# A graph block's edge sums: the overlap of two edge runs zeroed by one VectorE product per group instead of ScalarE copies

## The chip, the cores and the metric

The kernel runs on one core of a Trainium2 chip. The metric is the device time of one launch in microseconds (us), as the median of several runs. The core has five engines with queues of their own: TensorE (PE; its weight loads are shown as PEld), VectorE (DVE), ScalarE (ACT), GpSimd (POOL) and SyncE (SP). Each engine executes its own list of instructions strictly in order, and they meet at semaphores.

## The reference

There are 6250 nodes with 256 features and 106,250 edges with 96 features; the edges are sorted by their target node. For each node, the sum, the maximum and the mean of its edges' features are taken, put beside its normalised features and a global vector, and fed to a two-layer perceptron:

```
h = jnp.maximum(_layernorm(x, axis=-1), 0.0)
col = edge_index[1]
out1 = segment_sum(edge_attr, col)
cnt = segment_sum(ones, col)
out2 = where(cnt > 0, segment_max(edge_attr, col), 0)
out3 = out1 / maximum(cnt, 1.0)
z = concatenate([h, out1, out2, out3, u[batch]], axis=1)
y = relu(z @ W1 + b1) @ W2 + b2
out = x + (y + h)
```

## The kernel before, in words

**Tiles and groups.** The nodes are dealt to 49 tiles of 128 (one node to each partition), each partition's nodes being sorted by their number of edges, so that all 128 nodes of tile i have between LOW[i] and CAP[i] edges. A tile's edges are fetched by GpSimd as two runs, each with one indirect DMA (line 309): the first LOW edges of each node (k1 slots of 96 floats), and its last CAP - LOW edges (k2 slots). For a node with fewer than CAP edges the second run begins inside the first: those slots are the overlap. A table `mk` (128 x 49 x 20) holds 1 for slots of the second run that are new and 0 for slots of the overlap. For the maximum the overlap does no harm; for the sum it must be zeroed. One or two tiles with equal LOW and CAP form a group; there are 27 groups, 0 to 26. Edges lie in `ell` (all k1 + k2 slots), the zeroed copy of the second run in `es`; each has two buffers, by the group's parity, and both are named `work` in the trace.

**The overlap.** `mask` (lines 394 to 406) runs on ScalarE: for each of the n*k2 slots of a group (n tiles) one ACTIVATE Copy of 128x96 from `ell` to `es`, with the slot's column of `mk` as its scale (line 404). That makes 435 instructions, cut into pieces that stand between other work of ScalarE. The last one of a group signals `masked`.

**The trees.** `tree_head` on VectorE waits for `masked` (line 738) and adds the first run to `es` (line 743; in four tiles whose first run is shorter, line 748 also clears values for the maximum). `tree_mid` and `tree_tail` halve both buffers (line 754) until one sum and one maximum are left, in `cat`; the tail signals `tree_done`. GpSimd's `gather_group` waits for `tree_done` of group g before it issues the gathers of group g + 2 into the same buffer.

**The rest.** The 49 tiles form 14 batches of 2 to 4 tiles (1, 2 or 3 groups). ScalarE's `norm` and `means` fill the rest of `cat`. For each tile k of a batch TensorE transposes `cat` (line 523), ScalarE copies the result to `inh` (`in_hi`, line 440) and VectorE takes the rounding remainder `inl` (`in_lo`, line 843). TensorE then works at eight chunks (m = 0 to 7) of the hidden layer for the batch, `layer1` and, two chunks later, `layer2`; between them ScalarE does `relu` (lines 413 and 415) and VectorE `lo` (line 839).

**The order.** It is written by hand. A stage s has eight steps m. In it TensorE computes the chunks of batch s and, at the ends of chunks 2, 3, 5 and 6, transposes tiles 0, 1, 2 and 3 of batch b = s + 1; they are called k0 to k3 here. Transposes of one tile wait for `in_lo` of the tile before. VectorE at step m begins with `lo` of chunk m - 1 and then does: m = 0 and 1, mid and tail of the batch's first group; m = 2, `output` (line 865) and the head of the second group; m = 3, `in_lo` of tile 0 and mid; m = 4, `in_lo` of tile 1, tail, and the head of a third group; m = 5, the third group's mid and tail, and `moments` (line 810) of a batch ahead; m = 6, `in_lo` of tile 2 and `residual` (line 856); m = 7, `in_lo` of tile 3, `scales` (lines 822 to 832) and the head of the next batch's first group. ScalarE's pieces of `mask` come after `relu` of m = 0, 3, 4, 5, 6 and 7; for the next batch's first group they begin at m = 4 or 5, ahead of the step at which VectorE needs them.

The program has a branch for data that do not fit LOW and CAP (lines that begin with `general > 0`), which isn't taken.

Of the kernel before, what the change touches and what calls it, by code (L numbers as in the profile page):

```python
# [13 lines left out]
P = 128  # L14


def gnn_block(nc, x, dst, edge, u, W1, b1, W2, b2, out):
# [173 lines left out]
    x_in = [S(f"x_in{i}") for i in range(XS)]  # L191
    stored = [S(f"stored{i}") for i in range(XS)]
    ell_in = [S(f"ell_in{i}") for i in range(2)]
    masked, tree_done = S("masked"), S("tree_done")
    var_ready, std_ready, ln_done = S("var_ready"), S("std_ready"), S("ln_done")
    h_done, outs_done, over_done, trans_done = S("h_done"), S("outs_done"), S("over_done"), S("trans_done")
    hiT_done, loT_done, rem_hi, rem_lo = S("hiT_done"), S("loT_done"), S("rem_hi"), S("rem_lo")
# [33 lines left out]
    with nc.Block() as block:  # L231
# [136 lines left out]
        def _(act):  # L368
# [22 lines left out]
                act.wait_ge(var_ready, b + 1)  # L391
                act.activation(sd_[:, b % 2, 0:n], ve[:, b % 2, 0:n], ACT.Sqrt).then_inc(std_ready, 1)

            def mask(g, piece=0, pieces=1):

                a, n, k1, k2, _, _ = groups[g]
                if g == 0:
                    act.wait_ge(mask_ready, 1)
                if piece == 0:
                    act.wait_ge(ell_in[g % 2], ell_count(g))  # L400
                for at in range(n * k2 * piece // pieces, n * k2 * (piece + 1) // pieces):
                    j, e = at // k2, at % k2
                    src = (j * (k1 + k2) + k1 + e) * F
                    last = act.activation(es[g % 2][:, at * F:(at + 1) * F], ell[g % 2][:, src:src + F], ACT.Copy, scale=mk[:, a + j, e:e + 1])  # L404
                if piece == pieces - 1:
                    last.then_inc(masked, 1)

            def relu(C):
                cols = width(C // HC) * P
                m = C % HC  # L410
# [42 lines left out]
                    if k == width(b) - 1:  # L453
                        rem_in_hi(b)

            mask(0)
            root(0)
            for s in range(-1, NB):
                b = s + 1
                n, gs, ahead = width(b) if b < NB else 0, groups_in(b), groups_in(b + 1)  # L460
                for m in range(HC):
                    if m == 1:
                        for k in range(min(n, 1)):
                            norm(b, k)
                    if m == 2:
                        for k in range(1, min(n, 2)):
                            norm(b, k)
                        if n:
                            means(gs[0])
                    if m == 3:  # L470
                        in_high(b, 0)
                        for k in range(2, n):
                            norm(b, k)
                    if m == 4:
                        in_high(b, 1)
                    if m == 5 and len(gs) > 1:
                        means(gs[1])
                    if m == 6:
                        if len(gs) > 2:
                            means(gs[2])  # L480
                        in_high(b, 2)
                    if m == 7:
                        in_high(b, 3)
                    if s >= 0:
                        if s * HC + m == 0:
                            act.wait_ge(bias_set, 1)
                        relu(s * HC + m)
                    if m == 0 and len(gs) > 1:
                        mask(gs[1], 1, 2)
                    if m in (3, 4) and len(gs) > 2:  # L490
                        mask(gs[2], m - 3, 2)
                    if m == 6 and ahead:
                        root(b + 1)
                    first = 4 if len(gs) < 3 else 5
                    if first <= m < 7 and ahead:
                        mask(ahead[0], m - first, 7 - first)
                    if m == 7 and len(ahead) > 1:
                        mask(ahead[1], 0, 2)

        @block.tensor  # L500
        def _(pe):
# [85 lines left out]
        def _(dve):  # L587
# [146 lines left out]
            def tree_head(g):  # L734

                a, n, k1, k2, _, _ = groups[g]
                e, s = ell[g % 2], es[g % 2]
                dve.wait_ge(masked, g + 1)
                for lo in range(0, k1, k2):
                    w = min(k2, k1 - lo)  # L740
                    if lo:
# [204 lines left out]
```

## Time and profile before

| | before |
|---|---|
| median of 3 runs | 591.92 us (590.99 to 592.65) |
| time of the profiled execution | 595.76 us |
| its span, first to last instruction | 593.7 us |
| mean granted TensorE clock | 0.969 of full speed |
| VectorE | 846 instructions, 455.1 us busy |
| ScalarE | 935 instructions, 348.5 us busy |

The page counts as busy the time in which an engine executes an instruction. Each row of a timeline gives the start in the span, the duration, engine and line, the operation with its output and inputs, and in brackets how long the engine had been idle before and what ended that. Matmuls are pipelined, so the busy time of PE overstates its use; a row of PE with brackets shows a real pause.

### The profile page before, as it was taken

The numbers are of one execution on the slowest core, as the hardware profiler recorded it, in microseconds if no ns is written. First come the engines' busy times: TensorE is split into PE (matmuls) and PEld (weight loads), VectorE is DVE, ScalarE is ACT, GpSimd is POOL, SyncE is SP. The second block draws the span as 40 slices with busy tenths as digits, with TensorE's granted clock in tenths as the row PEclk, the third lists the DMA queues.
The fourth block names the chain that finished last, engine by engine and source line by source line (L and its number), as shares of the span: only waits on it lengthen the run. The fifth ranks groups of instructions, "written<-read, shape, count | busy, mean of one in ns | idle before, by whom it ended". The sixth has DMA issues, their size and how long they took to land. (4 is left out here: it accounts for less than half of the span.)

```text
span 593.7 us, 8528 instructions
## 1 busy us (share of the span) xinstructions
PE 493.6 (83%) x2937; PEld 434.0 (73%) x2937; DVE 455.1 (77%) x846; ACT 348.5 (59%) x935; POOL 246.2 (41%) x251
## 2 busy tenths in 40 slices
PE   0020669798999999999949999959999999999991
PEld 0020668788988888888848888848888888888991
DVE  4796758899896997969688969688959989792220
ACT  0844548675858767557737576747467576643330
POOL 3055530745466173561373751472751736102021
PEclk9999979999999999999987999989999999999996
DMA  2935440635534054440453440372560354000010
GB/s 62 289 97 163 130 141 2 223 123 162 184 118 146 7 206 159 127 160 3 167 190 139 137 161 11 141 228 107 163 216 25 138 205 135 27 2 35 1 36 18
DMA packets 18778, 71.03 MB, mean 120 GB/s; under 512 B 4577, under 2 KB 5699, under 8 KB 18720
## 3 DMA queue, kind: packets, MB, share of 16 engines
q0 software_dynamic: 15408, 65.72, 33.6%
q1 hardware_dynamic: 3322, 4.73, 2.7%
q8 instruction: 23, 0.38, 0.3%
q14 instruction: 25, 0.20, 0.1%
HBM read 64.03 MB, written 6.85 MB: 119 GB/s over the span
## 5 line engine op out<-in xcount | busy, mean ns | idle before, releaser
L309 POOL DMA_INDIRECT work<-in_edge_attr,idx x98 | 118.2, 1207 | 213.8 <-DVE cat L754 181.5
L538 PE MATMUL l1ps<-inh,w1h 128*128 128x512 f32 (+2 forms) x448 | 169.5, 384 | 0.8 <-ACT inh L440 0.8
L538 PE MATMUL l1ps<-inh,w1l 128*128 128x512 f32 (+2 forms) x448 | 164.9, 374 | 0.0
L754 DVE TENSOR_TENSOR work<-work 128x384 f32<-128x384 f32 (+17 forms) x174 | 151.5, 903 | 1.1
L404 ACT ACTIVATE work<-work,mk 128x96 f32<-128x96 f32 x435 | 122.1, 367 | 34.1 <-DMA work<-in_edge_attr,idx 33.8
L413 ACT ACTIVATE hf<-l1ps,b1e 128x512 f32<-128x512 f32 (+2 forms) x112 | 70.7, 631 | 119.8 <-PE l1ps L547 115.3
L839 DVE TENSOR_TENSOR hl<-hf,hh 128x512 fp32r<-128x512 f32 (+2 forms) x112 | 70.1, 626 | 55.4 <-ACT hh L415 46.4
L542 PE MATMUL l1ps<-inl,w1h 128*128 128x512 f32 (+2 forms) x448 | 111.7, 372 | 0.0
L323 POOL DMA_INDIRECT out_y<-xr,oidx x49 | 69.6, 1421 | 79.6 <-DVE xr L865 65.6
L561 PE MATMUL yps<-w2h,hh 128*128 128x256 f32 x392 | 99.7, 286 | 0.0
L561 PE MATMUL yps<-w2l,hh 128*128 128x256 f32 x392 | 98.0, 281 | 0.0
L538 PEld LDWEIGHTS l1ps<-inh,w1h 128*128 128x128 f32 x448 | 87.5, 195 | 12.3 <-issue 1.2
L538 PEld LDWEIGHTS l1ps<-inh,w1l 128*128 128x128 f32 x448 | 87.5, 195 | 11.3
L542 PEld LDWEIGHTS l1ps<-inl,w1h 128*128 128x128 f32 x448 | 80.9, 194 | 14.9
L561 PEld LDWEIGHTS yps<-w2h,hh 128*128 128x128 f32 x392 | 74.4, 190 | 7.9 <-issue 4.6
L561 PEld LDWEIGHTS yps<-w2l,hh 128*128 128x128 f32 x392 | 74.6, 190 | 3.0
L743 DVE TENSOR_TENSOR work<-work 128x1344 f32<-128x1344 f32 (+15 forms) x52 | 71.1, 1367 | 2.6 <-ACT work L404 1.7
L523 PE MATMUL tps<-ident,cat 128*128 128x128 f32 x196 | 32.1, 290 | 48.9 <-ACT cat L433 29.8
L415 ACT ACTIVATE hh<-l1ps,b1e 128x512 fp32r<-128x512 f32 (+2 forms) x112 | 70.1, 625 | 0.0
L302 POOL DMA_INDIRECT xr<-in_x,nid x49 | 53.6, 1095 | 36.4 <-DVE nid L661 21.8
L843 DVE TENSOR_TENSOR inl<-tps,inh 128x512 fp32r<-128x512 f32 x49 | 33.8, 689 | 43.5 <-ACT inh L440 32.7
L565 PE MATMUL yps<-w2h,hl 128*128 128x256 f32 x392 | 65.2, 283 | 1.5 <-DVE hl L839 1.5
(132 smaller groups left out, 463.5 us busy)
## 6 DMA issues: line engine op xcount, KB each, us to landing
work<-in_L_gnn_W SPq DMA_DIRECT2D x3, 1024.0 KB, 7.4
work<-in_edge_attr,idx POOLq DMA_INDIRECT x98
xr<-in_x,nid POOLq DMA_INDIRECT x49
out_y<-xr,oidx POOLq DMA_INDIRECT x49
work<-in_dst SPq DMA_DIRECT2D x1, 415.0 KB
dstp<-in_dst SPq DMA_DIRECT2D x1, 415.0 KB
work<-in_L_gnn_W SPq DMA_DIRECT2D x3, 128.0 KB, 7.5
xr<-in_L_gnn_W SPq DMA_DIRECT2D x1, 256.0 KB
```

The costliest lines, as they stand in the source:

```text
L309: pool.indirect_dma_start(out=ell[g % 2][:, at:at + kk * F], out_offset=None, in_=edge, in_offset=bass.IndirectOffsetOnAxis(ap=idx[:, a + ...
L323: pool.indirect_dma_start(out=out, out_offset=bass.IndirectOffsetOnAxis(ap=oidx[:, i:i + 1], axis=0), in_=xr[:, b % XS, k, :], in_offset=None,
L404: last = act.activation(es[g % 2][:, at * F:(at + 1) * F], ell[g % 2][:, src:src + F], ACT.Copy, scale=mk[:, a + j, e:e + 1])
L413: act.activation(hf[C % 2][:, 0:cols], l1ps[C % 2][:, 0:cols], ACT.Relu, bias=b1e[:, m:m + 1])
L415: act.activation(hh[C % 3][:, 0:cols], l1ps[C % 2][:, 0:cols], ACT.Relu, bias=b1e[:, m:m + 1]).then_inc(hi_done, 1)
L538: pe.matmul(ps, wt[:, c, ks(m)], inh[b % 2][:, c, 0:cols], start=(c == 0 and wt is w1h), stop=False)
L542: pe.matmul(ps, w1h[:, c, ks(m)], inl[b % 2][:, c, 0:cols], start=False, stop=False)
L561: pe.matmul(ybank(b, j)[:, j % 2 * D:(j % 2 + 1) * D], hh[C % 3][:, ks(j)], wt[:, m, :], start=False, stop=False, skip_group_check=True)
L565: last = pe.matmul(ybank(b, j)[:, j % 2 * D:(j % 2 + 1) * D], hl[C % 3][:, ks(j)], w2h[:, m, :], start=False, stop=(m == HC - 1), skip_gro ...
L743: V.tensor_tensor(out=slots(s, n, k2, 0, w), in0=slots(s, n, k2, 0, w), in1=slots(e, n, k1 + k2, lo, lo + w), op=ALU.add).then_inc(dve_ste ...
L754: return V.tensor_tensor(out=slots(buf, n, per, 0, size // 2) if out_ is None else out_, in0=slots(buf, n, per, 0, size // 2), in1=slots(b ...
L839: V.tensor_tensor(out=hl[C % 3][:, 0:cols], in0=hf[C % 2][:, 0:cols], in1=hh[C % 3][:, 0:cols], op=ALU.subtract).then_inc(lo_done, 1)
```

## The change

`mask` on ScalarE and its semaphore `masked` go, with all calls. `tree_head` on VectorE waits for the group's edges itself, and writes the zeroed second run into `es` with one `tensor_tensor` product for the whole group. Its first operand is the second run in `ell`, its second the group's columns of `mk`, each value read for 96 neighbours (a broadcast). The sum's first addition waits for that product through VectorE's own step semaphore. Nothing else is touched, and the other instructions keep their order on every engine.

```diff
-    masked, tree_done = S("masked"), S("tree_done")
+    tree_done = S("tree_done")
...
-            def mask(g, piece=0, pieces=1):
-
-                a, n, k1, k2, _, _ = groups[g]
-                if g == 0:
-                    act.wait_ge(mask_ready, 1)
-                if piece == 0:
-                    act.wait_ge(ell_in[g % 2], ell_count(g))
-                for at in range(n * k2 * piece // pieces, n * k2 * (piece + 1) // pieces):
-                    j, e = at // k2, at % k2
-                    src = (j * (k1 + k2) + k1 + e) * F
-                    last = act.activation(es[g % 2][:, at * F:(at + 1) * F], ell[g % 2][:, src:src + F], ACT.Copy, scale=mk[:, a + j, e:e + 1])
-                if piece == pieces - 1:
-                    last.then_inc(masked, 1)
...
-            mask(0)
             root(0)
...
-                    if m == 0 and len(gs) > 1:
-                        mask(gs[1], 1, 2)
-                    if m in (3, 4) and len(gs) > 2:
-                        mask(gs[2], m - 3, 2)
                     if m == 6 and ahead:
                         root(b + 1)
-                    first = 4 if len(gs) < 3 else 5
-                    if first <= m < 7 and ahead:
-                        mask(ahead[0], m - first, 7 - first)
-                    if m == 7 and len(ahead) > 1:
-                        mask(ahead[1], 0, 2)
...
-                dve.wait_ge(masked, g + 1)
+                if g == 0:
+                    dve.wait_ge(mask_ready, 1)
+                dve.wait_ge(ell_in[g % 2], ell_count(g))
+                V.tensor_tensor(out=s[:, 0:n * k2 * F].rearrange("p (n e f) -> p n e f", n=n, f=F),
+                                in0=e[:, 0:n * (k1 + k2) * F].rearrange("p (n e f) -> p n e f", n=n, f=F)[:, :, k1:k1 + k2, :],
+                                in1=mk[:, a:a + n, 0:k2, None].broadcast_to([P, n, k2, F]), op=ALU.mult).then_inc(dve_step, 1)
+                dve.wait_ge(dve_step, next(step))
```

VectorE at the end of the stage that prepares batch 4, from `in_lo` of its last tile on to the first `lo` of the next stage, before (`inr` is the remainder's third part, `r`, `rs` and `off` are `scales`):

```order
L843 TENSOR_TENSOR inl<-tps,inh 128x4x128
L848 TENSOR_TENSOR inr<-tpr,inr 32x512
L822 RECIPROCAL r<-std 128x4
...
L832 SCALAR_TENSOR_TENSOR off<-mv,rs 128x4
L743 TENSOR_TENSOR work<-work 128x2x192
L748 TENSOR_TENSOR work<-work,mb 128x1248 x2
L839 TENSOR_TENSOR hl<-hf,hh 128x512
```

The same place after the change (its line numbers are 18 lower from there on, and 24 lower for the product itself):

```order
L825 TENSOR_TENSOR inl<-tps,inh 128x4x128
L830 TENSOR_TENSOR inr<-tpr,inr 32x512
L804 RECIPROCAL r<-std 128x4
...
L814 SCALAR_TENSOR_TENSOR off<-mv,rs 128x4
L717 TENSOR_TENSOR work<-work,mk 128x2496
L725 TENSOR_TENSOR work<-work 128x2x192
L730 TENSOR_TENSOR work<-work,mb 128x1248 x2
L821 TENSOR_TENSOR hl<-hf,hh 128x512
```

The product of group 8 (26 slots, 2496 columns) stands between `scales` and the head's addition, and the next `lo` stands behind it. There is one such row for each of the 27 groups, with 1056 to 2496 columns.

ScalarE in the stage that prepares batch 7, steps 3 to 6, before:

```order
L404 ACTIVATE work<-work,mk 128x96 x10
L440 ACTIVATE inh<-tps 128x4x128
L413 ACTIVATE hf<-l1ps,b1e 128x512
L415 ACTIVATE hh<-l1ps,b1e 128x512
...
L404 ACTIVATE work<-work,mk 128x96 x7
L432 ACTIVATE cat<-cat,rc 128x64
L433 ACTIVATE cat<-cat,rc 128x96
L440 ACTIVATE inh<-tps 128x4x128
```

After the change:

```order
L426 ACTIVATE inh<-tps 128x4x128
L399 ACTIVATE hf<-l1ps,b1e 128x512
L401 ACTIVATE hh<-l1ps,b1e 128x512
...
L418 ACTIVATE cat<-cat,rc 128x64
L419 ACTIVATE cat<-cat,rc 128x96
L426 ACTIVATE inh<-tps 128x4x128
```

The pieces of `mask`, with their waits for gathered edges, no longer stand ahead of `in_hi`, `means` and `relu`.

## Rows read from the trace of the kernel before

**Rows 1.** The page: busy us (share of the span) and instructions of each engine.

```profile
PE 493.6 (83%) x2937; PEld 434.0 (73%) x2937; DVE 455.1 (77%) x846; ACT 348.5 (59%) x935; POOL 246.2 (41%) x251
```

**Rows 2.** Instructions by line and form: busy us, mean ns, idle before.

```profile
L404 ACT ACTIVATE work<-work,mk 128x96 f32<-128x96 f32 x435 | 122.1, 367 | 34.1 <-DMA work<-in_edge_attr,idx 33.8 <-issue 0.3
...
L748 DVE TENSOR_TENSOR work<-work,mb 128x1248 f32<-128x1248 f32 x2 | 2.9, 1458 | 0.1
...
L743 DVE TENSOR_TENSOR work<-work 128x1920 f32<-128x1920 f32 x2 | 4.3, 2154 | 0.2 <-ACT work L404 0.2
```

**Rows 3.** Windows: stretch, its length, busy us of the engines, clock, DMA share, GB/s.

```profile
120.00:140.00 20.00, 17.55 (x115) 16.70 (x115) 19.03 (x28) 13.04 (x36) 10.35 (x10) 1.00 0.50 167
...
300.00:320.00 20.00, 11.43 (x53) 9.67 (x52) 16.57 (x35) 8.22 (x25) 12.69 (x11) 0.74 0.73 243
```

**Rows 4.** Timeline of VectorE and ScalarE at the first group.

```profile
49.08 0.31 DVE L817 TENSOR_SCALAR ve<-mv 128x2 f32<-128x2 f32 x1
...
51.33 1.28 ACT L392 ACT_TABLE_LOAD   x1
...
52.85 0.17 DVE L822 RECIPROCAL r<-std 128x2 f32<-128x2 f32 x1 [3.47 <-ACT std L392]
```

**Rows 5.** Timelines, batches 1 to 3: two trees, `means` of group 3, k2.

```profile
71.43 2.15 DVE L743 TENSOR_TENSOR work<-work 128x1536 f32<-128x1536 f32 x2 [0.39 <-ACT work L404]
...
113.34 0.26 DVE L754 TENSOR_TENSOR cat<-work 128x96 f32<-128x96 f32 x1
...
114.35 0.33 ACT L432 ACTIVATE cat<-cat,rc 128x64 f32<-128x64 f32 x1
...
115.23 0.63 PE L523 MATMUL tps<-ident,cat 128*128 128x128 f32 x4 [2.13 <-ACT cat L433]
```

**Rows 6.** Timelines: k3 of batch 4, and on to k1 of batch 5.

```profile
187.55 0.60 PE L523 MATMUL tps<-ident,cat 128*128 128x128 f32 x4
...
190.79 0.60 ACT L440 ACTIVATE inh<-tps 128x512 fp32r<-128x512 f32 x1 [0.71 <-remote]
...
191.42 0.69 DVE L843 TENSOR_TENSOR inl<-tps,inh 128x512 fp32r<-128x512 f32 x1 [3.05 <-issue]
...
211.07 0.68 DVE L843 TENSOR_TENSOR inl<-tps,inh 128x512 fp32r<-128x512 f32 x1
...
211.90 0.63 PE L523 MATMUL tps<-ident,cat 128*128 128x128 f32 x4
```

**Rows 7.** Timelines, batch 7: mask pieces, `in_lo` of tile 1, a tree's end, k3.

```profile
289.82 2.77 ACT L404 ACTIVATE work<-work,mk 128x96 f32<-128x96 f32 x10 [0.58 <-DMA work<-in_edge_attr,idx]
...
293.11 0.69 DVE L843 TENSOR_TENSOR inl<-tps,inh 128x512 fp32r<-128x512 f32 x1 [3.08 <-ACT inh L440]
...
306.81 0.26 DVE L754 TENSOR_TENSOR cat<-work 128x96 f32<-128x96 f32 x1
...
308.55 1.97 ACT L404 ACTIVATE work<-work,mk 128x96 f32<-128x96 f32 x7 [9.86 <-DMA work<-in_edge_attr,idx]
...
312.37 1.08 PE L523 MATMUL tps<-ident,cat 128*128 128x128 f32 x4 [8.57 <-DVE inl L843]
```

**Rows 8.** Timeline of TensorE, batch 9: k3.

```profile
399.17 1.09 PE L523 MATMUL tps<-ident,cat 128*128 128x128 f32 x4 [6.78 <-DVE inl L843]
```

**Rows 9.** Timelines, batch 12: from `in_lo` of batch 11's tile 3 to k2.

```profile
480.58 0.69 DVE L843 TENSOR_TENSOR inl<-tps,inh 128x512 fp32r<-128x512 f32 x1 [1.20 <-issue]
...
509.98 0.36 DVE L754 TENSOR_TENSOR cat<-work 128x192 f32<-128x192 f32 x1
...
512.27 0.60 PE L523 MATMUL tps<-ident,cat 128*128 128x128 f32 x4
```

**Rows 10.** Timeline of TensorE: the last matmul of `layer1` in two chunks behind k2 of rows 5.

```profile
117.65 0.41 PE L547 MATMUL l1ps<-inr,w1r 96*128 96x256 f32 x1
...
120.98 0.28 PE L547 MATMUL l1ps<-inr,w1r 96*128 96x256 f32 x1
```

**Rows 11.** One line's instructions: GpSimd's edge gathers, duration ns min/median/max, first and last start.

```profile
L309 POOL DMA_INDIRECT work<-in_edge_attr,idx x98: 941/968/2932, 36.8 to 499.0; - x98
```

## The prediction, made blind

> **What bounds the kernel now.** The page first [rows 1]: TensorE is busy 83% of the span, VectorE 77%, ScalarE 59%. None is at 100%, so the shares do not decide; ScalarE has the most room and VectorE the least after TensorE. The chain that ended last breaks off at the last store, so it doesn't help. The table of stretches of 20 us is the next view. Two kinds stand out [rows 3]. From 100 to 150 us, where batches are small, VectorE has no idle time to speak of (19.0 of 20 us) while TensorE pauses: VectorE is the bound. From 160 us on TensorE is busy 20.00 of 20 us in almost every stretch: it is the bound there, with two holes, at 300 and at 380 us. So a microsecond added to VectorE costs a microsecond up to about 150 us, and later only what overruns TensorE's stage of about 38.6 us. The timelines then show what overruns it: VectorE works in one unbroken row from `in_lo` of a batch's last tile through the next batch's trees, and TensorE meets its results at the transposes k0 to k3.
>
> **What a product costs, and what goes.** ScalarE loses 435 activations, 122.1 us of busy time as listed, 34.1 us of idle time just ahead of them [rows 2]. VectorE gains 27 products over 435 x 96 = 41,760 columns. The nearest rows are products and sums of two SBUF operands, one of them with just such a broadcast: 1458 ns for 1248 columns (`mb`), 2154 ns for 1920 [rows 2]. The two give 1.036 ns a column and 165 ns fixed. Summed over the 27, 43.3 + 4.5 = 47.8 us, and with some 0.03 us between dependent instructions 48.6 us. For a single group that is 1.56 us (14 slots), 2.76 us (26 slots), and so on.
>
> A rule that speaks for the change would set this against the 122 us: the Trainium skill, VectorE: DVE Perf Modes, section "The TRN2 errata", says that VectorE and ScalarE pay a fixed latency for each instruction and that one large tile is better than many small ones. By that rule the machine's work falls by some 70 us. The trace agrees on the prices: 367 ns for 96 columns on ScalarE, 1458 ns for 1248 on VectorE [rows 2]. But ScalarE's time is mostly off the path, VectorE's is on it, so I do not sum by it.
>
> **Start (group 0).** Before, ScalarE masks group 0 first, then loads the table for Sqrt (1.28 us) and takes the root; VectorE's `scales` waits for it until 52.85 [rows 4]. Without the mask the load can follow `ve`, ready at 49.39: 49.4 + 1.28 + 0.2 gives 50.93, 1.9 us earlier. The product of group 0 (1.76 us, with its gap 1.8) stands between `scales` and the head. Net -0.1 us.
>
> **Batches 1 to 3 (70 to 150 us), groups 1 to 5.** VectorE is the bound. The five products are 1.76 + 1.56 + 1.26 + 1.56 + 1.56 = 7.7 us, with gaps 7.85. Against them, the wait of 0.39 us for ScalarE ahead of group 1's head goes [rows 5]. Group 3's tail ends at 113.60, but `means` begins at 114.35 behind a piece of the mask that had waited for gathered edges [rows 5]: some 0.65 us come back, and 0.45 us more where `inh` of that tile stood behind the next piece. Net 7.85 - 0.39 - 1.1 = **+6.35 us**.
>
> **Batches 4 to 6.** Take batch 5 [rows 6]. k3 of batch 4 ends at 188.26, but `inh` begins only at 190.79, since a mask piece of 2.50 us stood ahead of it on ScalarE; so `in_lo` comes at 191.42. Without the piece it comes at 188.95, 2.5 us earlier against TensorE. From there VectorE is never idle to the end of batch 5's first `in_lo`, 211.75; k1, which waits for it, begins at 211.90, a margin of 0.15 us. The products of groups 8 and 9 (26 and 20 slots) come between: 2.76 + 2.16 + gaps = 5.0. TensorE is pushed by 5.0 - 2.5 - 0.15 = 2.35 us. The same reading of batch 4 (its start can move by only 0.75 us) gives 1.9, of batch 6 0.85. Together **+5.1 us**.
>
> **Batches 7 and 9, the holes.** ScalarE waited 9.86 us for the edges of the next batch's first group, with `means` and `inh` behind it, and TensorE stood still for 8.57 us at k3 until `in_lo` of tile 2 [rows 7]. In the new order VectorE waits for these edges, three steps later, when they have landed; ScalarE is free. But the hole isn't empty on VectorE's side: it was working at group 14's tree until 307.07 [rows 7]. Now `in_lo` of tile 1, held until 293.11 by ScalarE [rows 7], can run at 290.7, group 13's tail then ends at 294.4; then come product 14 (2.2), its head (2.2), `lo` (0.6), mid and tail (7.35), `moments` (1.95), `lo` and `in_lo` (1.3): 310.0. k3 starts at 310.0 instead of 312.37, **-2.3 us**; TensorE still stands from 303.8 on. In batch 9 (hole of 6.78 us [rows 8]) the same steps end 1.7 us ahead of where k3 started, **-1.7 us**. Batches 8 and 10, which start from the late k3 of these, have margins larger than their products: 0.
>
> **Batches 11 and 12.** From `in_lo` at 480.58 (could be 480.15) VectorE idles 0.58 us in all until group 25's tail ends at 510.34; `means` adds 1.15 us, k2 is at 512.27 [rows 9], so the margin is 0.8. Products 24 and 25 cost 4.0. Push: 4.0 - 0.4 - 0.6 - 0.8 = 2.2 us. Batch 11 in the same way 1.5. **+3.7 us**. Batch 13 has a margin of over 3 us, and after it come no products.
>
> **The clock.** Behind TensorE's pause of 2.13 us at 115.23 [rows 5] the last matmul of a chunk shows 0.41 us, and 0.28 us one chunk later; the two are 3.33 us apart [rows 10], where a chunk of two tiles otherwise takes 2.2. That is the lower of the clock's two levels, 1.2 instead of 2.4 GHz, at a price of 1.1 us. New pauses of this size appear at batches 4, 5 and 12, and the one at 115 us gets shorter. I put one such price on the sum, +1 us, between 0 and +4.
>
> **Sum.** -0.1 + 6.35 + 5.1 - 4.0 + 3.7 + 1 = +12.0 us. Against the profiled execution's own time, 595.76, that is 607.8. The median of the runs shown is 3.8 us below that execution; I put the same difference on it: 591.92 + 12.0 = **603.9 us**. The bounds: if ScalarE's relief doesn't reach VectorE's starts (2.5, 0.75, 0.4 us and so on, 10 us in all), +22; if products run into margins that I read too small by 0.5 to 1 us each in the six batches that overrun, +7.
>
> **The rivals.**
> *A, the holes close and it gets faster.* ScalarE's waits of 33.8 us [rows 2] are the larger part of what was lost, and both holes go: -15.4 us instead of -4.0, with 2 us of slow clock behind them, so 12.0 - 11.4 - 2 = -1.4, and if batches 4 to 6 find slack too, -6.5: 586 to 590 us. For it: the rows name ScalarE's `inh` as what TensorE and VectorE wait for. Against it: VectorE's own tree of group 14. It decides at one point: whether `in_lo` of batch 7's tile 2 is done by 303.8 on the old scale, when TensorE arrives. 0.10. This is also where the rule on large tiles of the page above would lead.
> *B, all is covered.* ScalarE's relief and the margins just carry the products: 590.5 to 593.5. For it: VectorE's 23% of idle time. Against it: none of that lies between 94 and 150 us. 0.07.
> *C, every chain is longer by its whole products.* VectorE's start is not freed, because `in_lo` of the last tile then meets VectorE's own backlog: 591.9 + 22 = 614. Decides if `in_lo` of a last tile starts later than 0.8 us behind k3's end. 0.12.
> *D, GpSimd's issue is held up by the products.* Gathers' issues take 0.97 us but up to 2.93 us [rows 11], the long ones beginning inside long two-operand instructions of VectorE. With 27 more of them the edges land later by up to 2 us a time, and VectorE then waits at the head. It costs nothing until the landing passes the head; the smallest margin I find is 4.6 us (group 14: landed at 289.8, when ScalarE's wait for them ended [rows 7], needed at 294.4). If it is used up in two or three groups: +2 to +4 more, 607. 0.08. The Trainium skill, SBUF — State Buffer, section "Who interferes with whom", has such a rule: a VectorE instruction with two SBUF inputs contends with a GpSimd instruction that reads SBUF, not with one that only writes it. By that rule the indirect DMAs, which read their indices, would be held; no row here proves that this is the mechanism.
>
> **How the numbers follow.** The forecast has 0.63. Its own range is 598 to 609 us. With C's side the range for 8 in 10 is 597 to 612. A measurement here tells 0.3% (1.8 us) from no change. Faster than 590.1: A, 0.10. Within: B, 0.07. Slower than 593.7: forecast, C and D, 0.83.
>
> **What would show it.** Line 717 with 27 instructions, 47 to 49 us in all; VectorE near 502 us busy, ScalarE near 227 us. `scales` of batch 0 near 50.9 us, the first TensorE transposes of the loop where they were (61.9 us). k0 of batch 3 later by some 5 us, k1 of batch 5 by 10. `in_lo` of last tiles 0.7 us behind k3's end. The waits of ScalarE for edges gone, VectorE's for edges near zero; the holes still there, but 6 and 5 us wide, with VectorE working through them. Wrong it would be if the time between k1 of batch 5 and k1 of batch 13 isn't nearly the same as before, or if VectorE idles at line 717.

## The result and the profile after

The changed kernel takes 606.27 us (605.74 to 606.65, 4 runs) beside 592.28 us (590.99 to 593.11, 4 runs) for the kernel before on the same chip: ratio 1.0238 [1.0216, 1.0259], 14 us slower. The forecast was 603.9 us in a range of 597 to 612. The profiled execution of the changed kernel took 605.74 us, with a span of 604.0 us; its mean granted clock is 0.968.

Page of the changed kernel, busy us by engine:

```profile
PE 497.4 (82%) x2937; PEld 436.3 (72%) x2937; DVE 501.8 (83%) x873; ACT 236.9 (39%) x500; POOL 243.3 (40%) x251
```

Against [rows 1] ScalarE lost 111.6 us and VectorE gained 46.7. ScalarE lost less than the 122.1 us listed for its masks: for 10 us of those it was also executing a neighbouring activation, and that time stays busy without them (ScalarE's work other than masks is 236.6 us before and 236.9 after). The two together work 65 us less, and the kernel is 14 us slower. VectorE now shows a larger share than TensorE.

Instructions by line and form of the changed kernel (busy us, mean ns, idle before), three of the nine forms of line 717:

```profile
L717 DVE TENSOR_TENSOR work<-work,mk 128x1344 f32<-128x1344 f32 x11 | 17.1, 1556 | 0.0
L717 DVE TENSOR_TENSOR work<-work,mk 128x1536 f32<-128x1536 f32 x6 | 10.6, 1764 | 0.0
L717 DVE TENSOR_TENSOR work<-work,mk 128x1920 f32<-128x1920 f32 x3 | 6.5, 2151 | 0.4 <-issue 0.4
```

The nine forms add up to 47.7 us, forecast from [rows 2] as 47.8. Their idle time is next to nothing (0.5 us in all, none of it a wait for edges), so ScalarE's 33.8 us of waiting for them [rows 2] have no successor.

Single lines of the changed kernel (duration ns min/median/max, first and last start):

```profile
L309 POOL DMA_INDIRECT work<-in_edge_attr,idx x98: 937/991/2509, 36.3 to 508.0; - x98
```

The edge gathers' issues on GpSimd, 941/968/2932 in [rows 11], hardly changed: their sum is 119.9 us beside 118.2, the longest is shorter, and 19 rather than 14 of the 98 take over 1.5 us.

Waits of the changed kernel (engine, tile and line waiting, what it waits for: us in all, times, longest):

```profile
ACT cat L418 <- DVE cat L736: 77.0, 23, 8.2
...
PE tps L499 <- ACT cat L419: 32.9, 8, 19.8
PE tps L499 <- DVE inl L825: 21.5, 10, 6.5
...
DVE inl L825 <- ACT inh L426: 12.9, 20, 2.1
```

What TensorE's transposes wait for is a tree's end (`cat`, through `means`; 19.8 of these 32.9 us lie ahead of the first transposes) and `in_lo` (`inl`), both VectorE's. ScalarE now waits 77.0 us for trees, where it waited 29.4 before, and VectorE's wait for ScalarE's `inh` falls from 32.7 us to 12.9.

Windows of the changed kernel (columns as in [rows 3]; the columns behind ScalarE's and GpSimd's busy time are the granted clock, the DMA share and GB/s):

```profile
120.00:140.00 20.00, 16.65 (x97) 15.76 (x96) 19.03 (x28) 7.75 (x18) 10.52 (x9) 0.91 0.47 159
...
180.00:200.00 20.00, 20.00 (x110) 17.35 (x109) 16.15 (x34) 8.23 (x17) 9.92 (x9) 0.93 0.39 124
```

And of the kernel before, the second of these stretches:

```profile
180.00:200.00 20.00, 20.00 (x116) 17.44 (x115) 14.30 (x31) 18.35 (x59) 8.25 (x8) 1.00 0.35 107
```

Between 120 and 140 us VectorE is as full as before (19.03 us both times), but TensorE does 97 matmuls instead of 115 [rows 3], in 16.65 us instead of 17.55: the products push its work out of that stretch. In both stretches the clock was 1.00 before and is below it now.

The timelines give the running account. The table has the starts (us) of the transposes k0 to k3 of a batch, how much later they come than before (the lag), and the lag that the prediction's terms add up to:

| place | before | after | later by | forecast, without clock |
|---|---|---|---|---|
| batch 0, k0 | 61.89 | 60.15 | -1.74 | -0.1 |
| batch 3, k2 | 146.85 | 150.62 | +3.77 | +6.25 |
| batch 4, k1 | 173.10 | 179.27 | +6.17 | +8.15 |
| batch 4, k2 | 182.56 | 190.31 | +7.75 | +8.15 |
| batch 5, k1 | 211.90 | 222.01 | +10.11 | +10.5 |
| batch 6, k1 | 250.56 | 261.47 | +10.91 | +11.35 |
| batch 7, k3 | 312.37 | 321.23 | +8.86 | +9.05 |
| batch 9, k3 | 399.17 | 406.08 | +6.91 | +7.35 |
| batch 11, k2 | 473.58 | 482.12 | +8.54 | +8.85 |
| batch 12, k2 | 512.27 | 522.58 | +10.31 | +11.05 |
| end of the span | 593.7 | 604.0 | +10.3 | +11.0 |

Timelines of the changed kernel, all engines, from which the table's middle column and the readings below come:

```profile
32.05 1.04 ACT L380 ACTIVATE w1r<-work 96x1024 fp32r<-96x1024 f32 x1
...
36.07 1.28 ACT L392 ACT_TABLE_LOAD   x1
...
48.52 0.32 DVE L799 TENSOR_SCALAR ve<-mv 128x2 f32<-128x2 f32 x1
...
48.87 0.20 ACT L392 ACTIVATE std<-ve 128x2 f32<-128x2 f32 x1 [11.52 <-DVE ve L799]
...
60.15 1.09 PE L499 MATMUL tps<-ident,cat 128*128 128x128 f32 x4 [19.79 <-ACT cat L419]
...
150.62 0.63 PE L499 MATMUL tps<-ident,cat 128*128 128x128 f32 x4 [0.81 <-ACT cat L419]
...
179.27 0.84 PE L499 MATMUL tps<-ident,cat 128*128 128x128 f32 x4 [2.21 <-DVE inl L825]
...
180.54 0.63 PE L514 MATMUL l1ps<-inh,w1l 128*128 128x512 f32 x1
180.97 0.63 PE L514 MATMUL l1ps<-inh,w1h 128*128 128x512 f32 x1
...
190.31 0.60 PE L499 MATMUL tps<-ident,cat 128*128 128x128 f32 x4
...
195.30 0.60 PE L499 MATMUL tps<-ident,cat 128*128 128x128 f32 x4
...
196.68 0.69 DVE L825 TENSOR_TENSOR inl<-tps,inh 128x512 fp32r<-128x512 f32 x1 [0.60 <-ACT inh L426]
...
199.20 2.75 DVE L717 TENSOR_TENSOR work<-work,mk 128x2496 f32<-128x2496 f32 x1
...
214.82 2.15 DVE L717 TENSOR_TENSOR work<-work,mk 128x1920 f32<-128x1920 f32 x1
...
221.18 0.68 DVE L825 TENSOR_TENSOR inl<-tps,inh 128x512 fp32r<-128x512 f32 x1
...
222.01 0.63 PE L499 MATMUL tps<-ident,cat 128*128 128x128 f32 x4 [2.38 <-DVE inl L825]
...
310.54 6.50 DVE L736 TENSOR_TENSOR work<-work 128x1920 f32<-128x1920 f32 x8
...
317.86 1.41 DVE L792 BATCH_NORM_STATS2 stats<-xr 128x6 f32<-128x256 f32 x4
...
320.40 0.68 DVE L825 TENSOR_TENSOR inl<-tps,inh 128x512 fp32r<-128x512 f32 x1
...
321.23 1.09 PE L499 MATMUL tps<-ident,cat 128*128 128x128 f32 x4 [6.48 <-DVE inl L825]
...
406.08 1.08 PE L499 MATMUL tps<-ident,cat 128*128 128x128 f32 x4 [5.05 <-DVE inl L825]
```

The first row has a counterpart in the kernel before, work that the change does not touch:

```profile
32.59 1.04 ACT L380 ACTIVATE w1r<-work 96x1024 fp32r<-96x1024 f32 x1
```

The changed kernel's execution is thus 0.54 us ahead before anything that was edited: of the table's first lag, 0.54 us belong to the execution and 1.2 to the change (0.8 if held against the second profile of before, `base_again` below). The second profile of the changed kernel (`after_again`, below) has no such lead and its first transposes at 60.87.

The reader is to see three more things. At 196.68 `in_lo` of batch 4's tile 3 runs 0.78 us behind the end of k3's transposes (195.30 + 0.60), where before it ran 3.27 us behind [rows 6]. The same holds at the last tile of every batch from 3 to 12, where `in_lo` now comes 0.77 to 0.88 us behind (1.37 to 3.52 before): ScalarE's relief does reach VectorE. From there two products stand in VectorE's row before `in_lo` at 221.18, and TensorE, which had no pause at this place before [rows 6], waits 2.38 us for it. And the hole (TensorE's long pause at k3) of batch 7 is still 6.48 us wide while VectorE works through it: a tree's middle, the moments of a coming batch, then `in_lo`.

### The profile page after: what moved, and what is told of

Its sections match the earlier page's. It is cut to its first block and busy times, and to the rows that moved or that the text cites. A ratio compares the mean times of both kernels' runs of the same rounds, so it can differ in the third digit from the quotient of the medians.

```text
span 604.0 us, 8120 instructions
## 1 busy us (share of the span) xinstructions
PE 497.4 (82%) x2937; PEld 436.3 (72%) x2937; DVE 501.8 (83%) x873; ACT 236.9 (39%) x500; POOL 243.3 (40%) x251
## 5 line engine op out<-in xcount | busy, mean ns | idle before, releaser
L309 POOL DMA_INDIRECT work<-in_edge_attr,idx x98 | 119.9, 1224 | 227.4 <-DVE cat L736 196.9
L514 PE MATMUL l1ps<-inh,w1h 128*128 128x512 f32 (+2 forms) x448 | 171.4, 389 | 0.8 <-ACT inh L426 0.8
L323 POOL DMA_INDIRECT out_y<-xr,oidx x49 | 65.8, 1342 | 79.9 <-DVE xr L847 65.8
L514 PEld LDWEIGHTS l1ps<-inh,w1h 128*128 128x128 f32 x448 | 88.8, 198 | 12.5 <-issue 1.2
L514 PEld LDWEIGHTS l1ps<-inh,w1l 128*128 128x128 f32 x448 | 88.9, 198 | 11.4
L499 PE MATMUL tps<-ident,cat 128*128 128x128 f32 x196 | 33.3, 297 | 54.4 <-ACT cat L419 32.9
L499 PEld LDWEIGHTS tps<-ident,cat 128*128 128x128 f32 x196 | 24.0, 152 | 57.7 <-DVEq L786 33.6
L541 PEld LDWEIGHTS yps<-w2h,hl 128*128 128x128 f32 x392 | 54.0, 188 | 3.5 <-DVE hl L821 3.5
```

The lines of the kernel that those rows point to most:

```text
L309: pool.indirect_dma_start(out=ell[g % 2][:, at:at + kk * F], out_offset=None, in_=edge, in_offset=bass.IndirectOffsetOnAxis(ap=idx[:, a + ...
L323: pool.indirect_dma_start(out=out, out_offset=bass.IndirectOffsetOnAxis(ap=oidx[:, i:i + 1], axis=0), in_=xr[:, b % XS, k, :], in_offset=None,
L499: pe.transpose(tps[:, ks(c)], cat[:, k, ks(c)], ident[:, :])
L514: pe.matmul(ps, wt[:, c, ks(m)], inh[b % 2][:, c, 0:cols], start=(c == 0 and wt is w1h), stop=False)
L541: last = pe.matmul(ybank(b, j)[:, j % 2 * D:(j % 2 + 1) * D], hl[C % 3][:, ks(j)], w2h[:, m, :], start=False, stop=(m == HC - 1), skip_gro ...
```

## The experiments

Three series, each on one chip with its own runs of the kernel before: 595.37 us (591.74 to 598.3, 19 runs) in the first, 592.30 (591.1 to 594.45, 13) in the second, 592.93 (590.91 to 593.89, 21) in the third. Ratios are against these. Most kernels are mixtures, made from the kernel before by naming the groups that VectorE masks:

```diff
+BY_DVE = [0]
...
 def mask(g, piece=0, pieces=1):
+    if g in BY_DVE:
+        return
...
 def tree_head(g):
-    dve.wait_ge(masked, g + 1)
+    if g in BY_DVE:
+        dve.wait_ge(mask_ready, 1)
+        dve.wait_ge(ell_in[g % 2], ell_count(g))
+        V.tensor_tensor(out=s[:, 0:n * k2 * F].rearrange("p (n e f) -> p n e f", n=n, f=F),
...
+                        op=ALU.mult).then_inc(dve_step, 1)
+        dve.wait_ge(dve_step, next(step))
+    else:
+        dve.wait_ge(masked, sum(c not in BY_DVE for c in range(g + 1)))
```

### First series: the start, and the two halves of the change

**base_again**, the kernel before, unedited: was its profiled execution (595.76 us) unusual?

> The kernel before, unchanged, profiled once more. By its profile the change costs 604.0 - 593.7 = 10.3 us of span, by the medians 606.3 - 592.3 = 14.0 us. If the profiled execution of before happened to be a long one (a matter of that execution), this profile's span is near 590 us and a part of the kernel shows where the 3.5 us were. If the profiler itself makes before longer, the span is again 593 to 594 us.

Measured 594.84 us (593.61 to 598.1, 10 runs), 0.9995 [0.9973, 1.0018], span 592.9. The second profile agrees with the first. From its timelines:

```profile
308.82 1.97 ACT L404 ACTIVATE work<-work,mk 128x96 f32<-128x96 f32 x7 [10.03 <-DMA work<-in_edge_attr,idx]
...
312.64 1.09 PE L523 MATMUL tps<-ident,cat 128*128 128x128 f32 x4 [8.98 <-DVE inl L843]
```

The wait for edges and the hole are there again, somewhat longer than in [rows 7]. There is also a pause of 0.73 us at k1 of batch 5, where the first profile has none. So 595.76 was no outlier: this kernel's executions scatter over 591 to 598 us, and the median of three that stood beside the first profile was at their low end.

**only0**, VectorE masks group 0 alone (`BY_DVE = [0]`).

> Only group 0 is masked by VectorE, the other 26 as before. The theory after the result: ScalarE loads the table for Sqrt while it waits for the variance, so scales comes at 49.1 us and k0 of batch 0 1.7 us earlier than before; the gain is carried on because VectorE is the bound to 150 us: 590.5 us. The rival is the prediction's own step (the load begins only after the variance): -0.1 us, 592.2 us.

Measured 593.02 us (591.98 to 595.37, 10 runs), 0.9986 [0.996, 1.0012], span 590.7. Timeline:

```profile
60.80 1.09 PE L526 MATMUL tps<-ident,cat 128*128 128x128 f32 x4 [19.78 <-ACT cat L436]
```

The first transposes come 0.7 us earlier than in base_again (61.48) and 1.1 earlier than in the first profile of before. The table load runs at 36.72 us and the root at 49.52, as soon as the variance is there, with group 0's mask alone moved: the theory's step is shown. Of its 1.7 us 1.1 are there, since 0.5 were the lead of the first profile of after. The median is 2.35 us lower, but its interval includes no change.

**both**, ScalarE keeps its masks and VectorE makes the 27 products as well, each behind the mask of its group:

```diff
 def tree_head(g):
     dve.wait_ge(masked, g + 1)
+    V.tensor_tensor(out=s[:, 0:n * k2 * F].rearrange("p (n e f) -> p n e f", n=n, f=F),
...
+                    op=ALU.mult).then_inc(dve_step, 1)
+    dve.wait_ge(dve_step, next(step))
```

> ScalarE masks as before, and VectorE then does all 27 products on top (same values written again), so VectorE has its 48 us more and ScalarE no relief. If the relief of ScalarE is what holds the change's price down to 14 us (theory), this costs 20 to 28 us: 612 to 620 us, with in_lo of the last tiles again 2 to 3 us behind k3 and the pauses at batches 7 and 9 longer than before. If ScalarE's relief is worth nothing and the price is VectorE's work alone, 606 to 608 us.

Measured 630.25 us (626.96 to 631.47, 4 runs), 1.0584 [1.0534, 1.0635], span 628.1: above both expectations. Timelines:

```profile
330.22 1.97 ACT L405 ACTIVATE work<-work,mk 128x96 f32<-128x96 f32 x7 [9.34 <-DMA work<-in_edge_attr,idx]
...
335.14 1.08 PE L524 MATMUL tps<-ident,cat 128*128 128x128 f32 x4 [9.51 <-DVE inl L849]
...
424.75 1.09 PE L524 MATMUL tps<-ident,cat 128*128 128x128 f32 x4 [9.02 <-DVE inl L849]
```

k3 of batch 7 is 13.9 us later than in the changed kernel, k3 of batch 9 18.7 us, and both holes are wider than before (9.51 and 9.02 against 8.57 and 6.78 [rows 7, 8]), as expected. `in_lo` of the last tiles was expected 2 to 3 us behind k3: from batch 3 to 12 it comes 0.9 to 4.4 us behind.

**nomask**, neither masks nor products: the first sum of the head reads the gathered slots themselves, but for groups 8 and 9, whose product VectorE makes. In the other 25 groups edges of the overlap are counted twice, so this kernel's sums are not the reference's and it serves for its time alone:

```diff
+                dve.wait_ge(ell_in[g % 2], ell_count(g))
+                plain = k2 > k1
+                if plain:
...
-                    V.tensor_tensor(out=slots(s, n, k2, 0, w), in0=slots(s, n, k2, 0, w), in1=slots(e, n, k1 + k2, lo, lo + w), op=ALU.add).then_inc(dve_step, 1)
+                    V.tensor_tensor(out=slots(s, n, k2, 0, w), in0=slots(s, n, k2, 0, w) if lo or plain else slots(e, n, k1 + k2, k1, k1 + w), in1=slots(e, n, k1 + k2, lo, lo + w), op=ALU.add).then_inc(dve_step, 1)
```

> Neither ScalarE nor VectorE masks, except groups 8 and 9 by VectorE's product: the first addition takes the second run straight from the gathered buffer, so in the other 25 groups edges of the overlap are counted twice in the sum. The order is that of the changed kernel. Theory: start -3.5 us against before, groups 1 to 5 -1.5, batch 5 +2.4 (its products stay), hole of batch 7 -4.6, of batch 9 -3.6, together -11 us by the profile of before, some 3 us less by the medians: 582 to 586 us, with pauses of 3 to 5 us left at k3 of batches 7 and 9. If ScalarE's masks cost nothing before, 590 to 592 us.

Measured 584.65 us (583.07 to 584.71, 4 runs), 0.982 [0.9784, 0.9856], span 582.9. Timelines:

```profile
209.64 0.63 PE L526 MATMUL tps<-ident,cat 128*128 128x128 f32 x4 [2.36 <-DVE inl L853]
...
305.59 1.09 PE L526 MATMUL tps<-ident,cat 128*128 128x128 f32 x4 [4.04 <-DVE inl L853]
...
389.02 0.63 PE L526 MATMUL tps<-ident,cat 128*128 128x128 f32 x4 [3.44 <-DVE inl L853]
```

The pause of batch 5, where groups 8 and 9 have their products in this kernel too, has the 2.36 us that it has in the changed kernel (2.38). The holes stay at 4.04 and 3.44 us with no mask or product near them: that much of them is VectorE's other work.

Together the four cases, by the medians:

| | no products | products |
|---|---|---|
| masks on ScalarE | 595.4 (before) | 630.3 (both) |
| ScalarE relieved | 584.7 (nomask) | 606.3 (after) |

The changed kernel's median is from another series; the spans (593.7, 628.1, 582.9, 604.0) say the same within 1 us. The relief is worth 11 us where VectorE has no products (two of them are in that number) and 24 us where it has them; the products cost 35 us behind ScalarE's masks and 22 us without. So the two halves do not simply add: the change is one gain and one larger loss, and each depends by 13 us on whether the other is there.

### Second series: the products by stretch

**after_again**, the changed kernel once more.

> The changed kernel, unchanged, beside the kernel before on one chip. In 19 runs the kernel before came to 591.7 to 598.3 us with a median of 595.4, so the first comparison met it low. Theory: the change costs what the two profiles say, 10 to 12 us, and the changed kernel scatters less (605.5 to 607), since TensorE no longer waits for ScalarE's wait for gathered edges. Rival: the price is 14 us, 609 where before is 595.

Measured 606.2 us (606.03 to 607.37, 4 runs), 1.0244 [1.0224, 1.0263], span 604.3, with holes of 6.49 and 5.07 us. The price is 13.9 us: the theory's 10 to 12, taken from the two profiles, missed, and the rival's 14 came in. The theory's other half, that this kernel scatters little, held.

**early**, groups 1 to 5 (`BY_DVE = [1, ..., 5]`).

> VectorE masks groups 1 to 5 only (batches 1 to 3), ScalarE the rest. Theory: VectorE is the bound there, products 7.85 us less the 0.4 us wait and some relief: +5.5 to +6.4 us against before. Rival: the later stages have slack and take it up again: under +3 us.

Measured 598.68 us (597.78 to 599.41, 4 runs), 1.0115 [1.0098, 1.0132], span 596.0. +6.4 us, at the upper end of what was expected for these five products in the stretch that VectorE bounds. That later slack takes the loss up again is refuted. The hole of batch 7 has 7.37 us here:

```profile
312.19 1.97 ACT L407 ACTIVATE work<-work,mk 128x96 f32<-128x96 f32 x7 [8.65 <-DMA work<-in_edge_attr,idx]
...
316.01 1.09 PE L526 MATMUL tps<-ident,cat 128*128 128x128 f32 x4 [7.37 <-DVE inl L854]
```

**mid**, groups 6 to 11.

> VectorE masks groups 6 to 11 only (batches 4 to 6). In the changed kernel the lag between k2 of batch 3 and k1 of batch 6 grew by 7.1 us (3.8 to 10.9), where the prediction had 5.1. Theory: +5 to +7 us here, nothing of it made good later. Rival: without the backlog from batches 1 to 3, VectorE meets TensorE's stage with slack: under +3 us.

Measured 598.07 us (597.9 to 599.65, 4 runs), 1.0109 [1.0087, 1.013], span 596.2, so +5.8. Timelines, k1 of batches 4, 5 and 6, then ScalarE's wait for edges and the hole of batch 7:

```profile
174.79 0.63 PE L526 MATMUL tps<-ident,cat 128*128 128x128 f32 x4 [1.90 <-DVE inl L854]
...
216.00 0.63 PE L526 MATMUL tps<-ident,cat 128*128 128x128 f32 x4 [2.38 <-DVE inl L854]
...
255.45 0.63 PE L526 MATMUL tps<-ident,cat 128*128 128x128 f32 x4 [0.62 <-DVE inl L854]
...
312.10 1.97 ACT L407 ACTIVATE work<-work,mk 128x96 f32<-128x96 f32 x7 [8.48 <-DMA work<-in_edge_attr,idx]
...
315.92 1.08 PE L526 MATMUL tps<-ident,cat 128*128 128x128 f32 x4 [7.20 <-DVE inl L854]
```

Three pauses where TensorE had none in the first profile, 1.90, 2.38 and 0.62 us, against pushes of 1.9, 2.35 and 0.85 that the margins of the kernel before gave.

In early and mid the masks of batches 7 and 8 are still ScalarE's, and the hole of batch 7 follows ScalarE's wait for the edges: 9.86 and 8.57 us before, 10.03 and 8.98 in base_again, 8.65 and 7.37 in early, 8.48 and 7.20 in mid, the hole always 1.05 to 1.3 us the shorter. So in the kernel before it is ScalarE's wait that sets the hole's width, down to what VectorE's own row leaves.

**late**, groups 12 to 26.

> VectorE masks groups 12 to 26 only (batches 7 to 13). Theory: the two pauses shrink by some 2 us each, batches 11 and 12 cost 3.5: between -1.5 and +0.5 us against before. Rival (a price of VectorE's work alone, 27.5 us of products): +5 us or more.

Measured 593.38 us (592.23 to 594.45, 10 runs), 1.002 [1.0006, 1.0034], span 590.5. Timelines, k3 of batches 7 and 9:

```profile
308.82 1.09 PE L526 MATMUL tps<-ident,cat 128*128 128x128 f32 x4 [6.29 <-DVE inl L854]
...
392.95 1.09 PE L526 MATMUL tps<-ident,cat 128*128 128x128 f32 x4 [5.12 <-DVE inl L854]
```

+1.1 us by the medians, 0.6 above the upper end of what was expected (its interval, +0.4 to +2.0, takes that end in) and far from the rival's +5: 15 products, more than half, cost together next to nothing, since the holes give back what the last batches lose. In the traces the pauses of batches 11 and 12 come back here just as in the changed kernel, and the two batches lose 2.9 us (expected 3.5). The parts sum to 6.4 + 5.8 + 1.1, less 1 (by the timelines) to 2.35 (by the medians) for the start, which is 11 to 12.3 us; the whole is 13.9. The difference is of the size of the scatter of the kernel before, and what of it is an interaction stays open.

### Third series: a version that beats both

**holes**, only the two groups whose edges ScalarE waited for (`BY_DVE = [15, 20]`).

> VectorE masks only groups 15 and 20, the first groups of batches 8 and 10, whose edges land late; ScalarE no longer waits for them in the stages that prepare batches 7 and 9. Theory: the pauses at k3 there (7.2 to 9 and 6.7 us) shrink to what VectorE's own work sets, about 6.3 and 5.1 us, the two products are covered by the margins of batches 8 and 10: -2 to -4 us. Rival A of the prediction (ScalarE's waits are the whole pause): -13 to -15 us.

Measured 590.88 us (589.57 to 592.08, 12 runs), 0.9967 [0.9956, 0.9979], span 589.3. Timelines:

```profile
309.73 1.09 PE L526 MATMUL tps<-ident,cat 128*128 128x128 f32 x4 [6.68 <-DVE inl L854]
...
394.95 1.09 PE L526 MATMUL tps<-ident,cat 128*128 128x128 f32 x4 [5.84 <-DVE inl L854]
```

ScalarE's waits of 9.9 and 8.1 us are gone at the two places, and the holes shrink only from 8.57 and 6.78 us [rows 7, 8] (7.2 to 9.0 and 6.6 to 6.8 over the kernels above whose masks there are ScalarE's alone): the kernel gains 2 us, at the lower end of the 2 to 4 expected, and not the 13 to 15 of rival A.

**best_a**, group 0 on VectorE, and the mask that waited for edges stays on ScalarE but comes in one piece a step later:

```diff
-first = 4 if len(gs) < 3 else 5
+first = 4 if len(gs) < 3 else 6
```

> Group 0 is masked by VectorE, the rest by ScalarE, and in the stages with three groups the next batch's first group is masked in one piece at step 6, behind the third group's means and in_hi of tile 2. Theory: start -1 to -1.7 us; the pauses at batches 7 and 9 shrink to VectorE's own work, -2 and -1 us; with ScalarE's longer piece at step 6 covered. In all -3 to -5 us, below both kernels. Rival: the piece of 3.8 us at step 6 holds up in_hi of tile 3 and the next trees, and the gain is only the start's.

Measured 590.28 us (588.5 to 591.38, 10 runs), 0.996 [0.9945, 0.9975], span 589.0; holes 6.69 and 5.85 us, the same as in `holes`. It gains 2.65 us in all, less than the 3 to 5 expected. Taking the wait out of `inh`'s way works on either engine: what is left of the hole is not ScalarE's.

**best_c**, best_a, and in stages of three groups VectorE takes the moments behind `in_lo` of tile 2 instead of ahead of it:

```diff
     if m == 5:
...
-        if s + 2 < NB:
+        if s + 2 < NB and len(gs) < 3:
             moments(s + 2)
     if m == 6:
         in_low(b, 2)
+        if s + 2 < NB and len(gs) > 2:
+            moments(s + 2)
```

> As best_a, and in the stages with three groups moments (1.95 us of VectorE) comes behind in_lo of tile 2 instead of ahead of it. If VectorE's own row of work sets k3 there, as the reading of the hole says, the two pauses shrink by 1.9 us each more: 3 to 4 us below best_a. If something else holds TensorE there, no difference to best_a.

Measured 587.33 us (586.97 to 588.34, 6 runs), 0.9915 [0.9897, 0.9932], span 585.3. Timelines:

```profile
307.04 1.09 PE L526 MATMUL tps<-ident,cat 128*128 128x128 f32 x4 [5.24 <-DVE inl L854]
...
391.07 1.08 PE L526 MATMUL tps<-ident,cat 128*128 128x128 f32 x4 [4.11 <-DVE inl L854]
```

The holes shrink by another 1.45 and 1.74 us (expected 1.9 each), and the kernel by 2.95 against best_a. That shows by an edit of VectorE's order alone that VectorE's row sets what is left of the holes.

**best_d**, the same move of the moments, with groups 0, 15 and 20 on VectorE and `first` as it was.

> As best_c, but groups 15 and 20 are masked by VectorE at step 7 instead of by ScalarE at step 6 (with group 0). Theory: same pauses at k3; two products of 1.56 us come into VectorE's row where batches 8 and 10 have margins of over 1.5 us, and in_hi of tile 3 isn't held: within 1 us of best_c.

Measured 587.01 us (585.4 to 587.95, 6 runs), 0.9902 [0.9884, 0.9921], span 586.1; holes 5.24 and 4.10 us. It is faster than the kernel before by 5.9 us (1%) and than the changed kernel by some 19 (across series), and not to be told from best_c, as expected.

## Why the prediction was right, point by point

**The product's price: right.** 47.7 us for 27, forecast 47.8.

**The start: wrong.** The step "Without the mask the load can follow `ve`" failed. The load of the Sqrt table did not wait for the variance: it began at 36.07 us, right behind ScalarE's earlier work, and was over 11.5 us before the root. `scales` came at 49.11 instead of 50.9, and the first transposes 1.74 us earlier, not 0.1; 0.54 of that is the lead that this execution had anyway, 1.2 the change.

**Batches 1 to 3: mechanism right, size 0.85 us too high.** From batch 0 to k2 of batch 3 the lag grows by 5.5 us (-1.74 to +3.77), forecast 6.35; alone, these groups cost 6.4 by the medians, and early's traced lag grows by 5.2. Against base_again in place of the first profile the growth is 6.0, so part of the 0.85 is scatter. "VectorE has no idle time to speak of" was also read from one stretch: from 100 to 150 us it was busy 46.1 of 50 us. The sign "k0 of batch 3 later by some 5 us" missed with both errors: it came 2.19 us later.

**Batches 4 to 6: right.** The lag grows by 2.4, 2.36 and 0.8 us, forecast 1.9, 2.35 and 0.85 (k1 to k1; batch 4's clock loss apart, below); alone, mid shows 1.90, 2.38 and 0.62.

**The holes: right.** -2.05 and -1.95 us, forecast -2.3 and -1.7, with VectorE working through them. nomask, holes and best_c show from three sides that VectorE's row holds what is left of them. Above that floor ScalarE's wait sets the width, as early and mid show, so what the change gives back here depends on the execution of before that it is held against.

**Batches 8 and 10 at 0: right; 11 and 12: mechanism right, size 0.9 us too high.** No new pause of TensorE in batches 8 and 10. Of the +1.63 from batch 9's k3 to batch 11's k2 only 1.03 are batch 11's (forecast 1.5); 0.6 were lost directly behind batch 9's k3, without a new pause and at a granted clock of 0.87 over that stretch beside 0.90 before. Batch 12 lost 1.8 (2.2), and then nothing to the end.

**The clock: right kind, 0.6 us too low.** Between k1 and k2 of batch 4, behind the new pause of 2.21 us, 11.04 us pass instead of 9.46 (190.31 - 179.27 against 182.56 - 173.10), and the transposes at 179.27 themselves take 0.84 us where 0.63 is usual behind a short pause: the products of `layer1` behind them take 0.63 us until 182.7 and follow each other every 0.43 us, later 0.39 and every 0.23. That is the lower of the two levels, and the +1.6 us for which I had put +1. The pauses of batches 5 and 12, where I expected it too, show no such loss.

**The base: wrong, by 3.7 us.** Span against span the change costs 10.3 us, the forecast's 12.0 less 1.7 us. The start accounts for 1.6 of it (0.54 of that the execution's lead); the other misses (-0.85 in batches 1 to 3, +0.5 in 4 to 6, +0.6 for the clock, -0.3 from batch 9's k3 on) cancel, which is luck. The step "the median of the runs shown is 3.8 us below that execution; I put the same difference on it" failed. The changed kernel's profiled execution (605.74) lies 0.5 us below its median, and its executions stay within 605.7 to 607.4, while those of the kernel before spread over 7 us; a profile from the upper part of that spread says nothing on the changed kernel. Two errors of opposite sign, 3.7 us here and 1.6 us at the start, are why 603.9 came out only 2.4 us low: the mechanism was right stretch by stretch, but that the total came so near is in part luck.

**The upper bound: too low.** "If ScalarE's relief doesn't reach VectorE's starts" was priced at +22; both, where ScalarE keeps its masks and their waits, is the nearest case and shows +35. Of the 24 us between both and the changed kernel 12.3 lie in batches 4 to 6, 11 and 12, for which I had 10; the holes have 7.2, the start and batches 1 to 3 together 4.6, and for both of these I had put no loss.

**ScalarE's busy time: wrong.** 236.9 us, forecast 227. I took the listed 122.1 us off in full, 10 us of which it shared with other activations. Nothing hung on it.

**The rivals.** A fell with holes and best_a, at the point it named: `in_lo` of batch 7's tile 2 was not there when TensorE came. What was right in it is that ScalarE's wait sets the hole's width in the kernel before, but only down to VectorE's floor. The rule beside it, one large tile rather than many small ones (the Trainium skill, VectorE: DVE Perf Modes, "The TRN2 errata"), held for the engines' work, 65 us less, and not for the time. B fell with early and mid. C fell at its own point, 0.78 us instead of later than 0.8 behind k3, narrowly by the number but clearly by the 3.27 us of before; no later batch shows more than 0.88. D fell at VectorE: the products never wait for edges, and the gathers' issues take 2.51 us at most beside 2.93 before. The rule of the Trainium skill, SBUF — State Buffer, "Who interferes with whom", as the prediction applied it, would have these issues held more often. With 27 more two-operand instructions on VectorE their median rose from 968 to 991 ns and their sum by 1.7 us, so the trace shows a small growth at most, and no run isolates its cause.

## What to carry to other kernels

Two engines' busy time can fall by 65 us and the kernel be slower. The work came from an engine with room and went to one whose results the bound engine waits for; there each piece costs its full price less the margin at the next meeting point. Price such a move stretch by stretch, at the instructions where the engines meet, and count what the relief gives back separately; then mix, since here the gains came with groups 0, 15 and 20 alone, three of 27. A wait that sets the length of a pause may stand just above a second limit: taking 9.9 us of ScalarE's wait away shortened TensorE's pause by 2. And have the spread of a kernel's executions in hand before its profiled time is set against a median.

## What was not expected of the hardware

ScalarE executes the load of an activation table ahead of the wait of the activation that needs it: 36.07 us, while the activation itself waited for VectorE's `ve` until 48.87. In the kernel before, with masks ahead of it in the queue, the load stood behind them, at 51.33 [rows 4]. So here the change of function cost nothing where the engine was idle before it.

The two kernels scatter differently. Before: 591.7 to 598.3 us in one series, 590.9 to 593.9 in another. After: 605.7 to 607.4 over two. The two profiles of the kernel before differ in ScalarE's wait for the edges of batch 8's first group (9.86 and 10.03 us) and in the hole behind it (8.57 and 8.98). That the landing of edges, on which ScalarE waits in the one kernel and no engine in the other, makes the scatter fits this, and the hole following that wait in early and mid does too, but it was not shown: holes and best_a, without these two waits, still range over 2.5 and 2.9 us, and no experiment varied the landing alone.
